# Perceiver layer on one core: attention scores released bank by bank, weighted sums in two parts, a new deal of the key and value steps

## The chip, the cores and the metric

The kernel runs on one core of a Trainium2 chip, as one program. The metric is the device time of one execution in microseconds (us). The engines are named as in the profile: PE is the matrix engine (TensorE; PEld are its weight loads), DVE is VectorE, ACT is ScalarE, POOL is GpSimd, SP is the engine that issues most DMAs.

## What is computed

A layer of three residual parts, of which the change touches the first, cross attention of 64 queries to 1601 context rows in 32 samples, with 16 heads of 16 channels:

```python
q = split_heads(layernorm(x) @ Wq.T + bq)
k = split_heads(ctx @ Wk.T + bk)
v = split_heads(ctx @ Wv.T + bv)
attn = softmax(einsum('bhqd,bhkd->bhqk', q, k) * 4.0)
x = x + merge_heads(einsum('bhqk,bhkd->bhqd', attn, v)) @ Wp.T + bp
```

After it come a cosine circuit with a small feed-forward net and a mixture of seven routed experts and a shared one. They stand in the same program, behind the attention, and the change leaves them alone.

## The kernel before, in words

The attention works in 64 **periods** h, two for each of the 32 samples n = h // 2; a period handles 8 of the 16 heads (m = h % 2). All five engines run their own hand-written list of work for each period, and semaphores tie them together. Each period has four **quads** i = 0 to 3. A quad is what fits into the PSUM tile ps_s at once: four banks j of 128 x 401 scores.

What happens to a quad, engine by engine:

- PE, `scores(h, i)`, L903: 16 small products, which the array runs side by side as 32 x 32 tiles (32 matmul records), fill the four banks. Before the change PE waits until all four banks of the quad before have been read, and signals once.
- DVE, `take_scores`, L648: reads the four banks, scales them into the ring `probs` (5 slots) and leaves each row's extreme in `nmax`.
- After every second quad PE turns these extremes (`turn_max`, L923), DVE reduces them (`reduce_max`, L665), PE spreads the result over the partitions (`spread_max`, L930) and ACT copies it as a bias (`copy_bias`, L468).
- ACT, `exponentials`, L456: four exponentials, one for each bank, with that bias, in place in `probs`.
- DVE, `turn`, L670: one transpose of the quad into `pT`.
- POOL sums the rows (`less_extra`, L325, and `spread_sums`, L337).

When a period's four quads have been turned, PE forms the weighted sums of the values over 13 tiles (`weigh`, L937) and right behind them spreads the sums of the exponentials (L955 to L958, called spread below); DVE then divides (`normalise`, L679). Every fourth period has four normalised halves complete: PE projects them (`project_out`, L960) and DVE adds x and takes row statistics (`residual`, L698).

Meanwhile the keys and values of the next sample are made in 15 **steps** (`step`, L883): 8 K steps of 6 matmuls, 6 V steps of two tiles (12 matmuls) and V12 with one tile. A step fills one of two banks, ACT copies it out (`copy_steps`, L473). `STEP_ORDER` (L33) lists them, `steps_in` (L75) deals them to the four quarters of an even and an odd period. The input of a sample is loaded by SP (`load_ctx`, L239), and split in two parts by POOL (L303, L308). `FIRST_ORDER` and the first 14 steps serve the first sample, before the periods proper.

The order of the work is written out in the `period` functions of each engine: DVE L761, ACT L543, PE L1007, POOL L364, SP L259. On PE, which takes its queue in order, a period before the change reads:

```python
weigh(h - 1)
scores(h + 1, 1); steps[0]          # project_out within, every fourth period
turn_max(2 * h + 2); scores(h + 1, 2); steps[1]
spread_max(2 * h + 2); scores(h + 1, 3); steps[2]
turn_max(2 * h + 3); scores(h + 2, 0); steps[3]
spread_max(2 * h + 3)
```

On DVE a period reads, for i = 0 to 3: take_scores(h + 1, i); residual in i = 1 of every fourth period; turn(h, i); in i = 0 normalise(h - 1); in i = 1 and 3 reduce_max. The turns of i = 2 and 3 also wait for the weighted sums of h - 1, whose slots they use.

Of the kernel before, what the change touches and what calls it, by code (L numbers as in the profile page):

```python
# [16 lines left out]
NC = D // P  # L17
# [15 lines left out]
STEP_ORDER = [K(0, 0), K(0, 1), V(0), K(0, 2), V(2), K(0, 3), V(4), K(1, 0), V(6), K(1, 1), V(8), K(1, 2), V(10), K(1, 3), V(12)]  # L33
# [69 lines left out]
def attention_and_circuit(nc, ctxT, x, wq, bq, wk, bk, wv, bv, wp, rows, ident, marks, x1_scr, x1_mv, x1_by, x1_rs, x1_ex, w1, b1, w2, wr, rb, rows_scr,  # L103
                          wgu, wd, tri, counts):
    with ExitStack() as ctx:
# [132 lines left out]
        def _(sp):  # L238
# [20 lines left out]
            def period(h):  # L259
# [24 lines left out]
            sp.wait_ge(s_filled, HALF * NH)  # L284
# [17 lines left out]
        def _(pool):  # L302
# [13 lines left out]
            def own_queries(n):  # L316

                pool.wait_ge(q_ready_all, NC * (n // 8 + 1))
                if n > 1:

                    pool.wait_ge(s_filled, HALF * 2 * (n - 1))
                for e in range(2):
                    nc.gpsimd.tensor_scalar(q_own[:, n % 2, :, e, :], q_all[:, :, n * SQ:(n + 1) * SQ], mark[:, e:e + 1], None, ALU.mult).then_inc(q_owned, 1)
# [104 lines left out]
            pool.wait_ge(s_filled, HALF * NH)  # L428
# [26 lines left out]
        def _(act):  # L455
            def exponentials(h, i):  # L456
# [5 lines left out]
                for j in range(HALF):  # L462
# [10 lines left out]
            def copy_steps(steps):  # L473

                for n, s in steps:
# [3 lines left out]
                    if kind == "k":  # L479
                        m, q = of  # L480
                        if n > 0:

                            act.wait_ge(s_filled, HALF * (2 * (n - 1) + m + 1))
# [58 lines left out]

            def period(h):  # L543
# [11 lines left out]
                copy_steps(steps[1])  # L555
                if h + 1 < NH:
                    copy_bias(2 * h + 2)
                if h >= 0:
                    exponentials(h, 3)
                for i in ANGLES_IN.get((h, 3), ()):  # L560
                    angles(i)
                copy_steps(steps[2])
                if h + 1 < NH:
                    exponentials(h + 1, 0)
                copy_steps(steps[3])
# [81 lines left out]
        def _(dve):  # L647
            def take_scores(h, i):  # L648
# [3 lines left out]
                dve.wait_ge(s_filled, at + 1)  # L652
# [45 lines left out]
            def residual(t):  # L698
# [5 lines left out]
                nc.vector.tensor_tensor(x_t[:], ps_m[:, D:2 * D], x_t[:], ALU.add).then_inc(x1_ready, 1)  # L704
# [56 lines left out]
            def period(h):  # L761
                for i in range(HALF):
                    if h + 1 < NH:
                        take_scores(h + 1, i)
                    if i == 1 and h % 4 == 0 and h > 0:
# [3 lines left out]
                    if i == 0 and h > 0:  # L769
                        normalise(h - 1)  # L770
                    if i % 2 == 1 and h + 1 < NH:
                        reduce_max(2 * (h + 1) + i // 2)
                    if h == NH - 1:
                        for z in TURNS_IN[i]:
                            if z == 0:
                                dve.wait_ge(s_filled, HALF * NH)
# [99 lines left out]
        def _(pe):  # L876
# [26 lines left out]
            def scores(h, i):  # L903
# [8 lines left out]
                if at > 0:  # L912

                    pe.wait_ge(max_ready, HALF * at)
                else:
                    pe.wait_ge(q_ready_all, NC * NG)
                for g in range(QK):
                    for j in range(HALF):
# [18 lines left out]
            def weigh(h):  # L937

                n, m = h // 2, h % 2
                pe.wait_ge(turned, HALF * (h + 1))  # L940
                pe.wait_ge(kv_copied, STEPS * (n + 1))
                if h > 0:
                    pe.wait_ge(o_normed, h)
                for t in range(KT):
# [9 lines left out]
                mm.then_inc(o_filled, 1)  # L954
# [5 lines left out]
            def project_out(t):  # L960
                pe.wait_ge(o_normed, 4 * t + 4)
                pe.wait_ge(bias_ready, min(8 * t + 10, 2 * NH))
                for e in range(NC):
                    mm = nc.tensor.matmul(ps_m[:, D:2 * D], oT[:, e, :], wp_sb[:, e, :], start=(e == 0), stop=(e == NC - 1))
# [42 lines left out]
            def period(h):  # L1007
                steps = steps_in(h)
                if h > 0:
                    weigh(h - 1)  # L1010
                if h + 1 < NH:
                    scores(h + 1, 1)
                for z in steps[0]:
                    step(*z)
                    if h % 4 == 0 and h > 0 and z == steps[0][0]:
                        project_out(h // 4 - 1)
                if h % 4 == 0 and h > 0 and not steps[0]:
                    project_out(h // 4 - 1)
                if h % 4 == 0 and h > 0:

                    pe.wait_ge(x1_ready, h // 4)
                if h + 1 < NH:
                    turn_max(2 * h + 2)
                    scores(h + 1, 2)
                for z in steps[1]:
                    step(*z)
                if h + 1 < NH:
# [20 lines left out]
            for stage, g in PE_ORDER:  # L1048
                if stage == "weigh":
                    weigh(NH - 1)  # L1050
# [712 lines left out]
```

## Time and profile before

| | us |
|---|---|
| median of 3 runs | 1828.3 (1828.28 to 1830.08) |
| profiled execution, its own time | 1826.5 |
| its span, first to last instruction | 1824.6 |
| attention stage in it | 59 to 1302 |
| mean granted TensorE clock | 0.982 |

Busy over the whole span: PE 1652.9 us (91%), DVE 1566.3 (86%), ACT 1199.9 (66%), POOL 892.4 (49%). In the rows further down a timeline line has the start in us, the duration, engine, line, operation, output<-inputs and the number of instructions merged; a bracket gives the idle time of the engine before it and what ended it. Instructions of one engine overlap, so the distance of two starts, rather than a duration, says what an instruction costs its engine. Names: a_pss holds the scores, a_probs the ring, a_pT the turned quads, a_psm the extremes, a_pso the weighted sums, a_psk and a_psl the two step banks.

### The profile page before, as it was taken

How to read it: one execution, taken by the hardware profiler on the slowest of the kernel's cores; microseconds unless marked ns; L12 is line 12 of the kernel's file. 1: busy time of each engine (PE TensorE's matmuls, PEld its weight loads, DVE VectorE, ACT ScalarE, POOL GpSimd, SP SyncE). 2: the span in 40 equal slices, each digit the busy share in tenths (PEclk: the TensorE clock that was granted, in tenths of full speed). 3: DMA queues.
4: the chain of work that ended last, by engine and by line, in shares of the span. 5: the costliest groups of instructions: out<-in, count | busy, mean ns of one | idle time of the engine just before them, and what ended most of it. 6: DMA issues, size and time to landing. Idle time of an engine off the chain costs nothing. (4 is left out here: it accounts for less than half of the span.)

```text
span 1824.6 us, 59184 instructions
## 1 busy us (share of the span) xinstructions
PE 1652.9 (91%) x24272; PEld 1360.0 (75%) x24272; DVE 1566.3 (86%) x3585; ACT 1199.9 (66%) x3297; POOL 892.4 (49%) x1283
## 2 busy tenths in 40 slices
PE   7999999999999999999999999998499799999998
PEld 4776777767777677677767767766377799999998
DVE  5799999999999999999999999999886766666667
ACT  3676776776776776776776777777565345666652
POOL 5345444445445445444545444443321328888860
PEclk9999999999999999999999999999699899999999
DMA  4111111111111111211111211102012336666633
GB/s 168 40 43 43 64 43 43 61 43 43 64 43 43 61 43 43 64 43 43 62 42 43 64 43 43 53 33 93 6 59 78 136 115 215 211 227 229 214 125 116
DMA packets 43438, 147.86 MB, mean 81 GB/s; under 512 B 5680, under 2 KB 25008, under 8 KB 39712
## 3 DMA queue, kind: packets, MB, share of 16 engines
q1 hardware_dynamic: 38416, 130.71, 21.4%
q0 software_dynamic: 4752, 13.38, 2.4%
q8 instruction: 191, 3.13, 0.7%
q14 instruction: 79, 0.65, 0.1%
HBM read 129.78 MB, written 14.16 MB: 79 GB/s over the span
## 5 line engine op out<-in xcount | busy, mean ns | idle before, releaser
L465 ACT ACTIVATE a_probs<-a_probs,a_bias 128x401 f32<-128x401 f32 x1024 | 632.2, 625 | 0.0
L662 DVE TENSOR_SCALAR_CACHE_REDUCE a_probs<-a_pss 128x401 f32<-128x401 f32 x1024 | 527.8, 572 | 25.5 <-PE a_pss L919 14.9
L677 DVE STREAM_TRANSPOSE a_pT<-a_probs 128x1664 f32<-128x1664 f32 x256 | 487.3, 1904 | 0.0
L333 POOL TENSOR_SCALAR a_ex<-a_probs,a_marks 128x4 f32<-128x4 f32 x256 | 76.4, 299 | 636.7 <-ACT a_probs L465 636.5
L919 PE MATMUL a_pss<-a_keys,a_qown 32*32 32x401 f32 x8192 | 248.0, 509 | 14.2 <-DVE a_probs L662 13.5
L313 POOL TENSOR_TENSOR a_clo<-a_raw,a_chi 128x416 fp32r<-128x416 f32 x240 | 250.2, 1074 | 0.0
L953 PE MATMUL a_pso<-a_pT,a_v 128*32 128x128 f32 x6656 | 199.6, 278 | 10.7 <-DVE a_pT L677 10.7
L465 ACT ACTIVATION_READ_ACCUMULATOR a_probs<-a_probs,a_bias 128x1 f32 x1024 | 197.2, 193 | 0.0
L1592 PE MATMUL e_psg<-e_xh,e_guh 128*128 128x256 f32 x660 | 189.5, 287 | 5.7 <-DVE e_hl L1338 4.2
L953 PEld LDWEIGHTS a_pso<-a_pT,a_v 128*32 128x32 f32 x6656 | 181.7, 112 | 13.0 <-DVE a_pT L677 10.9
L1593 PE MATMUL e_psg<-e_xl,e_guh 128*128 128x256 f32 x660 | 186.6, 283 | 0.0
L1594 PE MATMUL e_psg<-e_xh,e_gul 128*128 128x256 f32 x660 | 186.4, 282 | 0.0
L1528 ACT ACTIVATE e_sg<-e_psg 128x256 f32<-128x256 f32 x180 | 69.1, 384 | 123.8 <-PE e_psg L1594 119.7
L1331 DVE TENSOR_TENSOR e_psg<-e_psg,e_sg 128x256 f32<-128x256 f32 x180 | 77.7, 432 | 80.4 <-ACT e_sg L1528 79.3
L484 ACT ACTIVATE a_keys<-a_psk,a_bk 128x401 f32<-128x401 f32 x131 | 77.4, 591 | 96.9 <-PE a_psk L881 96.9
L484 ACT ACTIVATE a_keys<-a_psl,a_bk 128x401 f32<-128x401 f32 x125 | 73.9, 592 | 95.2 <-PE a_psl L881 95.2
L1592 PEld LDWEIGHTS e_psg<-e_xh,e_guh 128*128 128x128 f32 x660 | 125.6, 190 | 6.4 <-issue 6.4
L1593 PEld LDWEIGHTS e_psg<-e_xl,e_guh 128*128 128x128 f32 x660 | 125.7, 191 | 0.0
L1594 PEld LDWEIGHTS e_psg<-e_xh,e_gul 128*128 128x128 f32 x660 | 125.6, 190 | 0.0
L879 PE MATMUL a_psl<-a_whi,a_chi 128*128 128x256 f32 x428 | 123.6, 289 | 0.0
L880 PE MATMUL a_psl<-a_wlo,a_chi 128*128 128x256 f32 x428 | 120.6, 282 | 0.0
L491 ACT COPY a_v<-a_psl 128x512 f32<-128x512 f32 x99 | 58.0, 586 | 94.9 <-PE a_psl L881 94.9
(246 smaller groups left out, 4299.7 us busy)
## 6 DMA issues: line engine op xcount, KB each, us to landing
a_raw<-in_ctxT SPq DMA_DIRECT2D x60, 832.0 KB, 4.6
f_gur<-in_wgu SPq DMA_DIRECT2D x24, 1408.0 KB, 6.2
f_dr<-in_wd SPq DMA_DIRECT2D x24, 768.0 KB, 4.7
e_big<-ys_scr SPq DMA_DIRECT2D x8, 512.0 KB, 7.7
a_probs<-in_ctxT SPq DMA_DIRECT2D x2, 1664.0 KB, 8.6
a_x<-in_x SPq DMA_DIRECT2D x16, 128.0 KB, 4.5
rows_scr<-f_a SPq DMA_DIRECT2D x8, 256.0 KB, 2.3
rows_scr<-f_a SPq DMA_DIRECT2D x4, 512.0 KB, 3.5
```

Source lines behind the costliest of these rows:

```text
L313: last = nc.gpsimd.tensor_tensor(out=c_lo[:, n % 2, k, cols], in0=src[:, cols], in1=c_hi[:, n % 2, k, cols].bitcast(F32), op=ALU.subtract)
L465: nc.scalar.activation(z, z, ACT.Exp, bias=bias[:, group % 4, at_bias:at_bias + 1], scale=-1.0, accum_out=esum[:, h % 2, j, 2 * e + r:2 * ...
L484: nc.scalar.activation(keys[:, m, q * KG:(q + 1) * KG], step_bank(at)[:, 0:KG], ACT.Identity, bias=bk_sb[:, m:m + 1]).then_inc(kv_copied, 1)
L662: nc.vector.tensor_scalar(probs[:, at % RING, j, 0:KG], ps_s[:, j, 0:KG], -SCALE, None, ALU.mult, ALU.min, accum_out=nmax[:, group % 2, at ...
L677: nc.vector.transpose(pT[:, turned_slot(h, i)].rearrange("p j k -> p (j k)"), probs[:, at % RING].rearrange("p j k -> p (j k)")).then_inc( ...
L879: nc.tensor.matmul(out, a[0], b[0], start=start, stop=False)
L880: nc.tensor.matmul(out, a[0], b[1], start=False, stop=False)
L919: mm = nc.tensor.matmul(ps_s[32 * g:32 * g + 32, j, 0:KG], q_own[32 * j:32 * j + 32, n % 2, m, e, 32 * r:32 * r + 32], keys[32 * j:32 * j ...
L953: mm = nc.tensor.matmul(ps_o[32 * j:32 * j + 32, 0:P], v_of(n)[:, t, 32 * p:32 * p + 32], moving, start=(t == 0), stop=(t == KT - 1))
L1592: nc.tensor.matmul(out, a[0], b[0], start=start, stop=False)
L1593: nc.tensor.matmul(out, a[0], b[1], start=False, stop=False)
L1594: return nc.tensor.matmul(out, a[1], b[0], start=False, stop=stop)
```

## The change

- `scores` goes bank by bank: the order of its loops is swapped, each bank waits only for the reading of the same bank of the quad before, and each bank signals. `s_filled` thus counts four per quad, and all that wait for it count in fours; `take_scores` waits bank by bank.
- `weigh` is split: 8 tiles behind scores 1, 5 tiles and the spread behind scores 2, one quarter later than before for the end.
- `normalise` and `residual` move from quads 0 and 1 to quad 2 on DVE, ahead of the turn; `residual` and `project_out` one period later, and their product to a free half of ps_o.
- `turn_max` moves from ahead of the scores to behind the scores and one step; `spread_max` behind the next scores.
- The steps are dealt 1, 2, 2, 3 and 1, 2, 2, 2 instead of 2, 2, 2, 2 and 2, 2, 2, 1, in a new `STEP_ORDER`.
- ACT does the four exponentials of a quad in two pairs, with a step's copy or the bias copy between them.
- SP stores the residual one period later.

```diff
-STEP_ORDER = [K(0, 0), K(0, 1), V(0), K(0, 2), V(2), K(0, 3), V(4), K(1, 0), V(6), K(1, 1), V(8), K(1, 2), V(10), K(1, 3), V(12)]
+STEP_ORDER = [K(0, 0), K(0, 1), K(0, 2), K(0, 3), V(0), V(2), K(1, 0), V(4), K(1, 1), K(1, 2), K(1, 3), V(6), V(8), V(10), V(12)]
+FIRST_TILES = 8
...
     elif h % 2 == 0:
-        plan = [[(n + 1, 1), (n + 1, 2)], [(n + 1, 3), (n + 1, 4)], [(n + 1, 5), (n + 1, 6)], [(n + 1, 7), (n + 1, 8)]]
+        plan = [[(n + 1, 1)], [(n + 1, 2), (n + 1, 3)], [(n + 1, 4), (n + 1, 5)], [(n + 1, 6), (n + 1, 7), (n + 1, 8)]]
     else:
-        plan = [[(n + 1, 9), (n + 1, 10)], [(n + 1, 11), (n + 1, 12)], [(n + 1, 13), (n + 1, 14)], [(n + 2, 0)]]
+        plan = [[(n + 1, 9)], [(n + 1, 10), (n + 1, 11)], [(n + 1, 12), (n + 1, 13)], [(n + 1, 14), (n + 2, 0)]]
...
-                if h % 4 == 0 and t >= 0:
+                if h % 4 == 1 and t >= 0:
 
                     sp.wait_ge(x1_summed, 2 * t + 2)
                     sp.dma_start(x1_scr[t], x_t[:]).then_inc(x1_free, 16)
...
                 if h >= 0:
-                    exponentials(h, 1)
+                    exponentials(h, 1, FORMER)
                     copy_bias(2 * h + 1)
+                    exponentials(h, 1, LATTER)
                 copy_steps(steps[0])
...
                 if h >= 0:
-                    exponentials(h, 2)
+                    exponentials(h, 2, FORMER)
+                copy_steps(steps[1][:1])
...
+                if h >= 0:
+                    exponentials(h, 2, LATTER)
+                copy_steps(steps[1][1:])
...
-                dve.wait_ge(s_filled, at + 1)
...
+                    dve.wait_ge(s_filled, HALF * at + j + 1)
                     nc.vector.tensor_scalar(probs[:, at % RING, j, 0:KG], ps_s[:, j, 0:KG], -SCALE, None,
...
-                    if i == 1 and h % 4 == 0 and h > 0:
+                    if i == 2 and h > 0:
+                        normalise(h - 1)
+                    if i == 2 and h % 4 == 1 and h > 4:
                         residual(h // 4 - 1)
                     if h >= 0:
                         turn(h, i)
-                    if i == 0 and h > 0:
-                        normalise(h - 1)
...
-                if at > 0:
-
-                    pe.wait_ge(max_ready, HALF * at)
-                else:
+                if at == 0:
                     pe.wait_ge(q_ready_all, NC * NG)
-                for g in range(QK):
-                    for j in range(HALF):
+                for j in range(HALF):
+                    if at > 0:
+
+                        pe.wait_ge(max_ready, HALF * (at - 1) + j + 1)
+                    for g in range(QK):
                         mm = nc.tensor.matmul(ps_s[32 * g:32 * g + 32, j, 0:KG], q_own[32 * j:32 * j + 32, n % 2, m, e, 32 * r:32 * r + 32],
                                               keys[32 * j:32 * j + 32, m, g * KG:(g + 1) * KG], start=True, stop=True)
-                mm.then_inc(s_filled, 1)
+                    mm.then_inc(s_filled, 1)
...
                 steps = steps_in(h)
-                if h > 0:
-                    weigh(h - 1)
+
                 if h + 1 < NH:
                     scores(h + 1, 1)
+                if h >= 0:
+                    spread_max(2 * h + 1)
                 for z in steps[0]:
                     step(*z)
...
+                if h > 0:
+                    weigh(h - 1, range(FIRST_TILES))
+
+                if h + 1 < NH:
+                    scores(h + 1, 2)
+                for z in steps[1][:1]:
+                    step(*z)
                 if h + 1 < NH:
                     turn_max(2 * h + 2)
-                    scores(h + 1, 2)
-                for z in steps[1]:
+                for z in steps[1][1:]:
                     step(*z)
+                if h > 0:
+                    weigh(h - 1, range(FIRST_TILES, KT))
+                    spread(h - 1)
+
                 if h + 1 < NH:
+                    scores(h + 1, 3)
                     spread_max(2 * h + 2)
-                    scores(h + 1, 3)
                 for z in steps[2]:
+                    step(*z)
+
+                if h + 2 < NH:
+                    scores(h + 2, 0)
+                for z in steps[3][:1]:
                     step(*z)
                 if h + 1 < NH:
                     turn_max(2 * h + 3)
-                if h + 2 < NH:
-                    scores(h + 2, 0)
-                for z in steps[3]:
+                for z in steps[3][1:]:
                     step(*z)
-                if h + 1 < NH:
-                    spread_max(2 * h + 3)
```

## Rows read from the trace of the kernel before

**Rows 1.** Busy time by engine in the attention stage; columns as in the first line.
```profile
core 0: us, PE busy (x) PEld busy (x) DVE busy (x) ACT busy (x) POOL busy (x), PEclk, DMA share, GB/s
59.00:1302.00 1243.00, 1127.25 (x20202) 870.05 (x20200) 1166.05 (x2711) 900.35 (x2654) 589.59 (x1016) 0.99 0.16 49
```
**Rows 2.** The same view, four consecutive periods.
```profile
629.47:648.00 18.53, 16.78 (x328) 12.73 (x320) 18.12 (x42) 13.73 (x41) 9.99 (x17) 1.00 0.15 49
648.00:667.96 19.96, 18.80 (x346) 14.90 (x339) 18.13 (x43) 14.44 (x42) 8.82 (x15) 1.00 0.16 51
668.00:686.50 18.50, 16.62 (x328) 12.57 (x313) 18.09 (x43) 13.73 (x41) 9.99 (x17) 1.00 0.16 49
686.50:707.90 21.40, 19.96 (x350) 15.56 (x340) 19.47 (x47) 14.43 (x42) 8.81 (x15) 1.00 0.16 48
```
**Rows 3.** Groups by line, 200 to 1200 us: busy, mean ns | idle before, releasers.
```profile
L687 DVE RECIPROCAL a_sT<-a_pso 128x128 f32<-128x128 f32 x51 | 48.8, 957 | 44.6 <-PE a_pso L953 40.1 <-issue 4.5
```
**Rows 4.** Timeline of DVE, two normalises and part of a period.
```profile
608.08 0.96 DVE L687 RECIPROCAL a_sT<-a_pso 128x128 f32<-128x128 f32 x1 [0.18 <-issue]
...
610.39 0.56 DVE L662 TENSOR_SCALAR_CACHE_REDUCE a_probs<-a_pss 128x401 f32<-128x401 f32 x1
...
629.47 0.96 DVE L687 RECIPROCAL a_sT<-a_pso 128x128 f32<-128x128 f32 x1 [1.60 <-PE a_pso L953]
...
637.81 1.91 DVE L677 STREAM_TRANSPOSE a_pT<-a_probs 128x1664 f32<-128x1664 f32 x1
639.88 0.58 DVE L662 TENSOR_SCALAR_CACHE_REDUCE a_probs<-a_pss 128x401 f32<-128x401 f32 x1 [0.16 <-DVE a_pT L677]
...
641.86 1.91 DVE L677 STREAM_TRANSPOSE a_pT<-a_probs 128x1664 f32<-128x1664 f32 x1
643.69 0.23 DVE L668 TENSOR_REDUCE a_low<-a_psm 8x32 f32<-8x128 f32 x1
```
**Rows 5.** Timeline of PE, the pieces of its queue.
```profile
610.52 1.13 PE L964 MATMUL a_psm<-a_wp,a_oT 128*128 128x256 f32 x4 [0.31 <-DVE a_oT L695]
611.30 0.47 PE L879 MATMUL a_psl<-a_whi,a_chi 128*128 128x256 f32 x1
...
612.81 0.28 PE L881 MATMUL a_psl<-a_whi,a_clo 128*128 128x256 f32 x1
...
625.91 0.24 PE L934 MATMUL a_psm<-a_id,a_low 8*32 8x8 f32 x8
626.08 3.05 PE L953 MATMUL a_pso<-a_pT,a_v 128*32 128x128 f32 x104
628.95 0.40 PE L957 MATMUL a_pso<-a_sin,a_marks 128*32 128x128 f32 x8
629.28 1.10 PE L919 MATMUL a_pss<-a_keys,a_qown 32*32 32x401 f32 x32
...
642.00 0.27 PE L928 MATMUL a_psm<-a_id,a_nmax 128*8 128x128 f32 x1 [1.01 <-DVE a_probs L662]
642.21 0.96 PE L919 MATMUL a_pss<-a_keys,a_qown 32*32 32x401 f32 x32
643.09 0.46 PE L879 MATMUL a_psk<-a_chi,a_whi 128*128 128x416 f32 x1
...
644.44 0.24 PE L934 MATMUL a_psm<-a_id,a_low 8*32 8x8 f32 x8
...
648.71 0.46 PE L879 MATMUL a_psl<-a_chi,a_whi 128*128 128x416 f32 x1
```
**Rows 6.** Timeline of ACT: an exponential, and the copy of a K step.
```profile
613.61 0.63 ACT L465 ACTIVATE a_probs<-a_probs,a_bias 128x401 f32<-128x401 f32 x1
...
650.18 0.60 ACT L484 ACTIVATE a_keys<-a_psl,a_bk 128x401 f32<-128x401 f32 x1 [2.54 <-PE a_psl L881]
```
**Rows 7.** Timeline of POOL: the second part of an input's split.
```profile
629.68 4.17 POOL L313 TENSOR_TENSOR a_clo<-a_raw,a_chi 128x416 fp32r<-128x416 f32 x4
```
**Rows 8.** DMA issues on the page: KB each, us to landing.
```profile
a_raw<-in_ctxT SPq DMA_DIRECT2D x60, 832.0 KB, 4.6
```
**Rows 9.** Timeline of PE's weight loads, those of one quad.
```profile
602.28 0.23 PEld L919 LDWEIGHTS a_pss<-a_keys,a_qown 32*32 32x32 f32 x32
```

More of the change, by code:

```diff
@@ L283, in _ @@
             sp.dma_start(x1[:, NT - 2, :], x1_scr[NT - 2]).then_inc(x1_loaded[group_of[-1]], 16)
-            sp.wait_ge(s_filled, HALF * NH)
+            sp.wait_ge(s_filled, HALF * HALF * NH)
             sp.dma_start(w1_raw, w1).then_inc(loaded, 16)
@@ L319, in own_queries @@
                 if n > 1:
-                    pool.wait_ge(s_filled, HALF * 2 * (n - 1))
+                    pool.wait_ge(s_filled, HALF * HALF * NC * (n - 1))
                 for e in range(2):
@@ L427, in _ @@
             less_extra(NH - 1, 1)
-            pool.wait_ge(s_filled, HALF * NH)
+            pool.wait_ge(s_filled, HALF * HALF * NH)
             pool.wait_ge(o_filled, NC * (B - 1))
@@ L455, in _, with exponentials @@
         def _(act):
-            def exponentials(h, i):
+            def exponentials(h, i, some=range(HALF)):
                 at = HALF * h + i
@@ L461, in exponentials @@
                 act.wait_ge(bias_ready, group + 1)
-                for j in range(HALF):
+                for j in some:
                     z = probs[:, at % RING, j, 0:KG]
@@ L541, in _ @@
             copy_steps([(0, s) for s in range(FIRST_STEPS)])
+            FORMER, LATTER = range(HALF // 2), range(HALF // 2, HALF)
             def period(h):
@@ L558, in period @@
                 if h >= 0:
-                    exponentials(h, 3)
+                    exponentials(h, 3, FORMER)
+                copy_steps(steps[2][:1])
+                if h >= 0:
+                    exponentials(h, 3, LATTER)
                 for i in ANGLES_IN.get((h, 3), ()):
                     angles(i)
-                copy_steps(steps[2])
+                copy_steps(steps[2][1:])
                 if h + 1 < NH:
-                    exponentials(h + 1, 0)
-                copy_steps(steps[3])
+                    exponentials(h + 1, 0, FORMER)
+                copy_steps(steps[3][:1])
+                if h + 1 < NH:
+                    exponentials(h + 1, 0, LATTER)
+                copy_steps(steps[3][1:])
             for h in range(-1, NH):
@@ L775, in period @@
                             if z == 0:
-                                dve.wait_ge(s_filled, HALF * NH)
+                                dve.wait_ge(s_filled, HALF * HALF * NH)
                             round_turns(z)
@@ L935, in spread_max, with weigh @@
                 mm.then_inc(max_spread, 1)
-            def weigh(h):
+            def weigh(h, some):
                 n, m = h // 2, h % 2
-                pe.wait_ge(turned, HALF * (h + 1))
-                pe.wait_ge(kv_copied, STEPS * (n + 1))
-                if h > 0:
-                    pe.wait_ge(o_normed, h)
-                for t in range(KT):
+                if some.start == 0:
+                    pe.wait_ge(turned, HALF * (h + 1))
+                    pe.wait_ge(kv_copied, STEPS * (n + 1))
+                    if h > 0:
+                        pe.wait_ge(o_normed, h)
+                    if h % 4 == 1 and h > 4:
+                        pe.wait_ge(x1_ready, (h - 1) // 4)
+                for t in some:
                     for j in range(HALF):
@@ L953, in weigh, with spread @@
                         mm = nc.tensor.matmul(ps_o[32 * j:32 * j + 32, 0:P], v_of(n)[:, t, 32 * p:32 * p + 32], moving, start=(t == 0), stop=(t == KT - 1))
-                mm.then_inc(o_filled, 1)
+                if some.stop == KT:
+                    mm.then_inc(o_filled, 1)
+            def spread(h):
                 pe.wait_ge(sums_spread, h + 1)
@@ L961, in project_out @@
                 pe.wait_ge(o_normed, 4 * t + 4)
-                pe.wait_ge(bias_ready, min(8 * t + 10, 2 * NH))
                 for e in range(NC):
-                    mm = nc.tensor.matmul(ps_m[:, D:2 * D], oT[:, e, :], wp_sb[:, e, :], start=(e == 0), stop=(e == NC - 1))
+                    mm = nc.tensor.matmul(ps_o[:, D:2 * D], oT[:, e, :], wp_sb[:, e, :], start=(e == 0), stop=(e == NC - 1))
                 mm.then_inc(y_filled, 1)
@@ L1049, in _ @@
                 if stage == "weigh":
-                    weigh(NH - 1)
+                    weigh(NH - 1, range(KT))
+                    spread(NH - 1)
                     pe.wait_ge(loaded, 16 * 7)
```

16 lines of the change are left out of this document (6 added, 10 removed).

## The prediction

> **What bounds the kernel now.** I read the busy time of the long middle stretch first. It is the attention stage, 59 to 1302 us: VectorE (DVE) is busy for 1166 of its 1243 us, TensorE (PE) for 1127, ScalarE for 900 [rows 1]. Two engines lie within a few per cent of the bound, so neither can lose time without the other noticing. Next I cut four periods out of the middle, from one normalise to the next: 18.53, 19.96, 18.50 and 21.40 us, 78.39 together, with the granted clock at 1.00, 2.4 GHz [rows 2]. This pattern repeats to the end of the stage. Then I asked the groups where DVE's idle time lies: nearly all in front of the reciprocal that opens normalise, 44.6 us in 1000 [rows 3]. The timeline shows how: it waits 1.60 us in one period and 0.18 in the next, in turn [rows 4].
>
> **The DVE's own work.** From the timeline [rows 4], with t = 0 where the last bank of a quad of scores has been read and the turn starts: turn to reduce 1.83 (641.86 to 643.69), reduce 0.23, reading four banks 1.98 to 1.99 (639.88 to 641.86), turn directly to a reading 2.06 to 2.07 (637.81 to 639.88), normalise 2.31 (608.08 to 610.39). The new order in a period is read, turn, read, turn, reduce, read, normalise, turn, read, turn, reduce: 1.99 + 2.06 + 1.99 + 1.83 + 0.23 + 1.99 + 2.31 + 2.06 + 1.99 + 1.83 + 0.23 = 18.51 without waiting. Residual adds 21.40 - 19.96 = 1.44 to every fourth period [rows 2]. So moving normalise and residual removes no work: all that can change is what DVE waits for.
>
> **PE's pieces**, start to start [rows 5]. A quad of scores takes 0.88 (642.21 to 643.09); a K step before work of another tile shape 1.35 (643.09 to 644.44); a V step after other work 1.51 to its twelfth matmul (611.30 to 612.81) and, an estimate from K's last matmuls, 0.12 more to the next step or 0.19 to 0.2 to another shape, so 1.63 or 1.70. V12 has six of the twelve: about 1.00. Turn_max 0.21 (642.00 to 642.21), spread_max 0.17 to 0.19, the weighted sums 2.87 for 13 tiles (626.08 to 628.95), so 1.77 for eight and 1.10 for five, spread 0.33, project_out 0.78. Hand-overs: PE starts 0.14 after DVE's last read (641.86 [rows 4], 642.00); DVE starts normalise 0.52 after spread's start (628.95, 629.47), and reduce 0.39 after turn_max's (its 0.27 and the same 0.12).
>
> **Does this bookkeeping hold?** Tried on the kernel before: t = 0, turn_max 0.14, scores 0.35, one K step 1.23, spread_max 2.58, weigh 2.76, spread 5.63, normalise could start at 6.15; DVE reaches it at 1.83 + 0.23 + 1.99 + 1.91 = 5.96. Wait 0.19, seen 0.18. With K and V in that quarter everything is 1.5 later and the wait is 1.6, seen 1.60 [rows 4]. It gives both periods to a few hundredths.
>
> **The change, walked through.** Decisive is PE's new queue between the scores that wait for quad 3 and the spread that normalise needs. PE runs in order. *Odd period* (t = 0 as above): scores' last bank starts at 0.14; the next step 0.81 later (an estimate: a quad's 0.88 to 0.90 less the hundredths that issuing three banks takes), K10 at 0.95; turn_max 2.30; V4 2.50; K11 4.13; scores of quad 1 at 5.38, spread_max 6.28, K12 6.47; eight tiles of weigh 7.82; scores of quad 2 at 9.69; K13 10.59; turn_max 11.94; V6 12.14; five tiles 13.84; spread 14.94. DVE: reduce is due at 1.83 but can start at 2.69, a wait of 0.86 that before was none, since turn_max then stood ahead of the scores. Read, turn, read, turn: due at the second reduce at 10.79, turn_max gives 12.33, wait 1.54. Then reading ends at 14.55, spread gives 15.46, wait 0.91. Sum 3.31, period 18.51 + 3.31 = 21.82. *Even period*: last bank 0.14, V12 0.95, turn_max 1.95 (reduce waits 0.51), K00 2.15; PE is ready for quad 1 at 3.50 but its last bank is read only at 4.56; so K01 at 5.70, weigh 7.05, quad 2 at 8.92, K02 9.82, turn_max 11.17 (reduce waits 1.12), K03 11.37, five tiles 12.72, spread 13.82 (normalise waits 0.56). Sum 2.19, period 20.70. Where project_out stands ahead of weigh, 0.85 with its change of shape comes onto this path; residual adds its 1.44, so that period is 24.11. Four periods: 21.82 + 20.70 + 24.11 + 20.70 = 87.33, against 78.39: 8.94 more.
>
> After normalise comes the other side of the bad deal: DVE needs 2.31 + 2.06 + 1.99 before quad 3 is read, while PE has one quad, spread_max and two steps, about 4.2, and then idles; nothing of the weighted sums can be pulled into that hole.
>
> **Edits with no price.** *Bank-wise signals*: the last bank is filled as late as before (0.14 behind its read). Three more waits per quad on either engine: between 0 and about 0.08 each (a reading's accumulator pass exposed); taken as 0, since a turn, which waits too, follows a read at the banks' own pace (0.50). If the upper end held on the path, +30 us; if spread_max ran wholly under the scores, 0.19 a period less, -12. *Exponentials in twos*: the same instructions of 0.63 [rows 6]; a K copy can start 1.47 after its step (648.71 [rows 5] to 650.18). The tightest turn is quad 1's in the odd period: its last exponentials, now behind the bias copy, end near 8.6, its reading at 8.96. Cover 0.4; without it, the 1.54 wait behind would absorb more. Quad 3's is covered by about 2. *K00 of the next sample*: its split input comes from POOL's 4.17 us after quad 1's exponentials [rows 7], some 10 us earlier. *SyncE*: the store of a residual now stands behind one more input load and in front of the next; that next load goes out about 6 us later than its buffer allows, near 21 of 24, and with 4.6 to land [rows 8] it is there 2 us before POOL asks. Covered; otherwise POOL alone would slip.
>
> **Weighing a rule.** The new order of a bank sends four matmuls in a row to the same 32 rows of the array. Before, the fifth load already goes to rows in use: all 32 loads are over within 0.23 us while the matmuls run on to 0.96 [rows 5, 9], so loads do run under matmuls of their own rows. I take 0.88 for a quad. The Trainium skill, "TensorE: Matmul & The Clock Gate", section "Part 3: Packing small matmuls", says that a weight load overlaps matmuls in flight only when they use another row group. By it every bank would be serial; the trace disagrees.
>
> **The sum.** Full periods are h = 1 to 61: 61/4 x 8.94 = 136 us. The first two periods lack the sums, the last two the steps (there turn_max directly follows the scores and nothing waits longer): +-4. The stages after 1302 don't change. The profiled execution took 1826.5 (span 1824.6): 1962.5; the median of the runs is 1.8 above it: 1964.
>
> **Rivals.** (1) *Faster*: DVE never waits, because bank-wise starts put PE ahead. Place: spread must start before 12.15 - 0.52 = 11.63 after t = 0 (DVE's own work to the normalise). PE has 14.8 of work ahead of it, so it would need some 3.2 us of it to run beneath other work, as if steps didn't wait for scores to drain. Then four periods take 4 x 18.51 + 1.44 = 75.5, -2.9: -44 us, 1784. Against: the step starts 0.88 behind the scores. 4%. (2) *No change*: bank by bank is idle, and later sums and later normalise cancel: 1828. Against: 12.5 to 14.8 us of PE work must fit into 11.5. 3%. (3) *Milder*: steps run shorter or spread_max and the split sums hide, a third to two thirds of the loss: 1870 to 1915. The bookkeeping above speaks against it. 7%. (4) *Packing breaks*: four matmuls of about 0.5 one behind another in each bank, banks side by side: +1.2 a quad, five a period, +290: 2250 at least, more if banks are serial too. Against: [rows 9]. 2%. It is what that rule of the Trainium skill would do. (5) *Worse waiting*: each bank's wait costs on both engines, or the granted clock, 1.00 (2.4 GHz) in all four periods [rows 2], falls to its lower level with PE's longer idling: above 2005. 5%. The forecast has the remaining 79%.
>
> **Numbers.** 1964. Range 1905 to 2005: from the walk's bounds (about 1930 to 2000) out to the upper part of the milder case. What a measurement here can tell from no change is about 0.2%, 4 us. Slower 93%, the same 3%, faster 4%.
>
> **What the profile after should show.** Periods of about 20.7 and 21.8 in turn, 24.1 every fourth; the attention stage near 1379 us; DVE's share of it down from 94 to about 85%. In front of reduce, where before shows no wait [rows 4], some 125 to 140 us over the run, ended by turn_max; in front of the reciprocal still about 45, now in every period. Quads as dense as before. PE idle in front of the scores of quad 0. Wrong would be: reduce not waiting, normalise waiting less than 0.3 on average, or a quad longer than 1 us without a wait.

## The result, and the profile after

The changed kernel takes 1905.3 us (median of 4 runs, 1902.8 to 1907.0) against 1828.3 before: a ratio of 1.042, 95% interval 1.040 to 1.044. Slower by 77 us, as forecast in sign, where 136 were forecast. The profiled execution shown here took 1902.76 us, with a span of 1900.9.

The windows, first the attention stage, then four periods from normalise to normalise (they answer to [rows 1, 2]):

```profile
core 0: us, PE busy (x) PEld busy (x) DVE busy (x) ACT busy (x) POOL busy (x), PEclk, DMA share, GB/s
61.57:1376.95 1315.38, 1252.92 (x20190) 922.04 (x20166) 1140.09 (x2710) 894.76 (x2646) 590.95 (x1015) 0.97 0.14 47
...
777.36:797.80 20.44, 20.00 (x346) 15.27 (x338) 17.66 (x42) 14.31 (x42) 9.42 (x17) 1.00 0.15 51
797.80:817.10 19.30, 18.86 (x328) 13.11 (x321) 17.67 (x42) 13.73 (x41) 9.47 (x17) 1.00 0.14 48
817.10:838.42 21.32, 20.88 (x350) 16.04 (x342) 17.67 (x43) 14.31 (x42) 9.42 (x17) 1.00 0.08 34
838.42:859.19 20.77, 18.87 (x328) 13.11 (x320) 19.03 (x47) 13.73 (x41) 9.46 (x17) 1.00 0.20 61
```

The stage went from 1243 to 1315 us and carries 72 of the 76 us between the two spans. Four periods at full clock take 81.83 instead of 78.39 [rows 2], 3.44 more; over 61 periods that is 61/4 x 3.44 = 52 us. The clock of the whole stage fell from 0.99 to 0.97, while these four periods show 1.00: the other 20 us of the stage go with stretches at a lower clock, which the first experiment tests. Look also at DVE: 17.66 us of work in a period where before had 18.1, although the change was to take no work from it.

The waits of DVE over the whole span (total, times, longest):

```profile
DVE a_low L684 <- PE a_psm L944: 130.2, 126, 8.2
...
DVE a_sT L703 <- PE a_pso L973: 34.3, 60, 0.7
```

The new wait is where it was forecast: reduce (a_low) waits for turn_max in every period, 130.2 us in all (forecast 125 to 140). That the sum falls into the forecast is luck, as the account below shows. The reciprocal (a_sT) waits in all periods instead of every second one.

Now one odd period on PE, the one that has project_out. The quad of scores that begins at 821.56 runs with DVE's reads, bank by bank; the last read that it waits for ends at 822.82, where the DVE lines below begin. That is t = 0 of the prediction's walk.

```profile
821.56 2.27 PE L935 MATMUL a_pss<-a_keys,a_qown 32*32 32x401 f32 x32 [0.44 <-DVE a_probs L678]
823.76 0.46 PE L895 MATMUL a_psl<-a_chi,a_whi 128*128 128x416 f32 x1
...
825.02 0.27 PE L944 MATMUL a_psm<-a_id,a_nmax 128*8 128x128 f32 x1
825.04 0.36 PE L895 MATMUL a_psk<-a_whi,a_chi 128*128 128x256 f32 x1
...
826.55 0.36 PE L895 MATMUL a_psl<-a_chi,a_whi 128*128 128x416 f32 x1
...
827.81 0.96 PE L935 MATMUL a_pss<-a_keys,a_qown 32*32 32x401 f32 x32
828.50 0.45 PE L950 MATMUL a_psm<-a_id,a_low 8*32 8x8 f32 x8
828.88 0.46 PE L895 MATMUL a_psk<-a_chi,a_whi 128*128 128x416 f32 x1
...
830.14 1.03 PE L987 MATMUL a_pso<-a_wp,a_oT 128*128 128x256 f32 x4
831.09 1.95 PE L973 MATMUL a_pso<-a_pT,a_v 128*32 128x128 f32 x64
832.98 0.97 PE L935 MATMUL a_pss<-a_keys,a_qown 32*32 32x401 f32 x32
833.88 0.46 PE L895 MATMUL a_psl<-a_chi,a_whi 128*128 128x416 f32 x1
...
835.15 0.27 PE L944 MATMUL a_psm<-a_id,a_nmax 128*8 128x128 f32 x1
835.17 0.36 PE L895 MATMUL a_psk<-a_whi,a_chi 128*128 128x256 f32 x1
...
836.78 1.30 PE L973 MATMUL a_pso<-a_pT,a_v 128*32 128x128 f32 x40
837.89 0.40 PE L981 MATMUL a_pso<-a_sin,a_marks 128*32 128x128 f32 x8
```

And what DVE does in it (turn, the two reduces, normalise, residual's first add):

```profile
822.82 1.91 DVE L693 STREAM_TRANSPOSE a_pT<-a_probs 128x1664 f32<-128x1664 f32 x1
...
825.33 0.28 DVE L684 TENSOR_REDUCE a_low<-a_psm 8x32 f32<-8x128 f32 x1 [0.60 <-PE a_psm L944]
...
835.46 0.28 DVE L684 TENSOR_REDUCE a_low<-a_psm 8x32 f32<-8x128 f32 x1 [2.04 <-PE a_psm L944]
...
838.42 0.96 DVE L703 RECIPROCAL a_sT<-a_pso 128x128 f32<-128x128 f32 x1 [0.71 <-PE a_pso L973]
839.41 0.48 DVE L707 SCALAR_TENSOR_TENSOR a_op<-a_pso,a_marks,a_sT 128x64 f32<-128x64 f32 x2
839.92 0.29 DVE L711 SCALAR_TENSOR_TENSOR a_oT<-a_op,a_bv 128x64 f32<-128x64 f32 x1
840.13 0.42 DVE L717 TENSOR_TENSOR a_x<-a_x,a_bp 128x256 f32<-128x256 f32 x1
```

Three things are to be seen. Normalise waits for the spread at 837.89, which stands behind PE's whole queue, in the order that was walked. The step of V behind turn_max starts 0.02 after it (825.02, 825.04; 835.15, 835.17), where the walk had 0.20, and then takes 1.61 up to the weighted sums (835.17 to 836.78), where the walk had 1.70. And normalise takes 840.13 - 838.42 = 1.71, where the walk had 2.31. The whole difference there is its last instruction, shown by the groups from 200 to 1200 us (busy, mean ns | idle before it):

```profile
L711 DVE SCALAR_TENSOR_TENSOR a_oT<-a_op,a_bv 128x64 f32<-128x64 f32 x48 | 13.8, 287 | 1.7
```

The same group of the kernel before:

```profile
L695 DVE SCALAR_TENSOR_TENSOR a_oT<-a_op,a_bv 128x64 f32<-128x64 f32 x51 | 45.5, 892 | 1.8
```

892 ns before, 287 after, for the same instruction. The timeline of before shows what ran beside it: POOL's split of an input, four instructions of 1.04.

```profile
608.29 4.16 POOL L313 TENSOR_TENSOR a_clo<-a_raw,a_chi 128x416 fp32r<-128x416 f32 x4
...
609.58 0.89 DVE L695 SCALAR_TENSOR_TENSOR a_oT<-a_op,a_bv 128x64 f32<-128x64 f32 x1
```

POOL's second instruction ends near 608.29 + 2.08 = 610.37, and the DVE instruction, begun about a quarter of the way into it, ends at 609.58 + 0.89 = 610.47, some 0.1 behind it. By the single records it is 0.08 to 0.09 in each of the 52 periods from 200 to 1250 us that have such a split. The two instructions ahead of it, which read one operand from PSUM, keep their 0.48. In the changed kernel normalise comes two quads later, when POOL is through with the split: no period there has the two side by side.

The lower clock is the other finding. The windows around one hole of PE:

```profile
1007.60:1009.50 1.90, 0.03 (x1) 0.00 (x0) 1.79 (x4) 1.90 (x6) 1.19 (x3) 1.00 0.79 216
1009.50:1011.30 1.80, 1.76 (x30) 0.64 (x32) 1.80 (x7) 0.26 (x2) 0.36 (x1) 1.00 0.80 318
1011.30:1014.70 3.40, 3.40 (x20) 2.53 (x11) 2.13 (x5) 0.94 (x3) 0.00 (x0) 0.51 0.00 0
1014.70:1025.50 10.80, 10.80 (x223) 7.60 (x238) 9.50 (x27) 7.92 (x25) 7.30 (x12) 1.00 0.11 23
```

PE stands idle for 1.90 us ahead of the scores of quad 0, while DVE does normalise, residual, a turn and reads; it works again from 1009.5, and from 1011.3 to 1014.7 the granted clock is 0.51, the 1.2 GHz level. Such a hole comes in every fourth period. Leaving out the last 35 us of the stage, where the steps have run out and both kernels fall to the lower level, the trace holds 18 stretches at that level, 68.3 us together (called low stretches below); the trace of before holds none. Not every hole is followed by one: behind 11 of the 14 holes a low stretch begins 0.8 to 3.0 us after work has resumed, behind three there is none, and seven low stretches lie further from any hole.

### The profile page after: what moved, and what is told of

It reads as the page before. It is cut to its first block and busy times, and to the rows that moved or that the text cites. A ratio compares the mean times of both kernels' runs of the same rounds, so it can differ in the third digit from the quotient of the medians.

```text
span 1900.9 us, 59183 instructions
## 1 busy us (share of the span) xinstructions
PE 1785.4 (94%) x24272; PEld 1417.8 (75%) x24272; DVE 1541.1 (81%) x3585; ACT 1197.6 (63%) x3297; POOL 893.6 (47%) x1283
## 5 line engine op out<-in xcount | busy, mean ns | idle before, releaser
L935 PE MATMUL a_pss<-a_keys,a_qown 32*32 32x401 f32 x8192 | 366.2, 514 | 52.1 <-DVE a_probs L678 51.4
L935 PEld LDWEIGHTS a_pss<-a_keys,a_qown 32*32 32x32 f32 x8192 | 98.1, 103 | 189.6 <-DVE a_probs L678 108.7
L973 PE MATMUL a_pso<-a_pT,a_v 128*32 128x128 f32 x6656 | 212.9, 279 | 7.3 <-DVE a_pT L693 7.3
L684 DVE TENSOR_REDUCE a_low<-a_psm 8x32 f32<-8x128 f32 x128 | 35.6, 278 | 130.3 <-PE a_psm L944 130.2
L895 PE MATMUL a_psl<-a_whi,a_chi 128*128 128x256 f32 x412 | 128.3, 311 | 0.0
L895 PE MATMUL a_psk<-a_whi,a_chi 128*128 128x256 f32 x420 | 127.4, 303 | 0.0
```

What stands on the lines that cost most here:

```text
L895: nc.tensor.matmul(out, a[0], b[0], start=start, stop=False)
L973: mm = nc.tensor.matmul(ps_o[32 * j:32 * j + 32, 0:P], v_of(n)[:, t, 32 * p:32 * p + 32], moving, start=(t == 0), stop=(t == KT - 1))
```

## The experiments

Theory: the 77 us are 52 at full clock, from PE's queue in front of the waits of reduce and normalise (already less what the change gains unasked where normalise leaves POOL's split), plus some 20 of the lower clock that goes with the holes. Rivals: bank by bank costs the time itself; the pairs of exponentials do; the lower clock changes nothing that counts. Periods named below run from the turn of one quad 3 to that of the next (t = 0 of the walk); they are odd, even, odd with residual, the medians at full clock. The changed kernel has 20.45, 19.30, 22.78.

**Fill the hole.** In the periods with residual, four products into an unused part of ps_m ahead of the scores of quad 0:

```diff
+                if h % 4 == 1 and h > 4:
+                    pe.wait_ge(bias_ready, 2 * h + 3)
+                    for _ in range(4):
+                        nc.tensor.matmul(ps_m[:, D:2 * D], a_id_sb[:], wp_sb[:, 0, :], start=True, stop=True)
                 if h + 2 < NH:
                     scores(h + 2, 0)
```

> The changed kernel with four extra matmul calls on PE (their product is used by nobody) in the 1.9 us hole ahead of quad 0's scores, in the periods with a residual. Theory (the stretches at 1.2 GHz that the changed kernel shows follow these holes and cost some 20 us): about 10 or fewer such stretches remain instead of 21, and 1880 to 1895. Rival (they lie off the path or have another cause): 1905, or a few us more where the filler delays the scores.

1885.6 us, ratio 1.031 (1.029 to 1.032): 19.7 us faster than the change, with more work. The periods at full clock stay at 20.45, 19.30 and 22.78; of the 18 low stretches 4 are left, 13.7 us, and no hole of 0.9 us or more. The clock from 330 to 1330 us, first of this kernel and then of the changed one:

```profile
330.00:1330.00 1000.00, 981.50 (x15826) 719.70 (x15825) 877.47 (x2096) 682.35 (x2022) 455.04 (x779) 1.00 0.15 47
```

```profile
330.00:1330.00 1000.00, 960.96 (x15358) 710.62 (x15357) 862.05 (x2060) 671.89 (x1986) 450.22 (x768) 0.97 0.14 47
```

So filling the holes takes away 54.6 us at the lower level and 19.7 us of time, with the periods at full clock unchanged: the holes bring most of the low stretches about, those further off included, and a microsecond at the lower level costs about 0.36 us here. The 57 us that are left are the 52 at full clock and what the four remaining stretches cost. What brings those four about is not shown.

**Deal two steps behind the spread.** K03 and V6 go from ahead of the last five tiles to the quarter behind them; everything else stays:

```diff
-        plan = [[(n + 1, 1)], [(n + 1, 2), (n + 1, 3)], [(n + 1, 4), (n + 1, 5)], [(n + 1, 6), (n + 1, 7), (n + 1, 8)]]
+        plan = [[(n + 1, 1)], [(n + 1, 2)], [(n + 1, 3), (n + 1, 4), (n + 1, 5)], [(n + 1, 6), (n + 1, 7), (n + 1, 8)]]
-        plan = [[(n + 1, 9)], [(n + 1, 10), (n + 1, 11)], [(n + 1, 12), (n + 1, 13)], [(n + 1, 14), (n + 2, 0)]]
+        plan = [[(n + 1, 9)], [(n + 1, 10)], [(n + 1, 11), (n + 1, 12), (n + 1, 13)], [(n + 1, 14), (n + 2, 0)]]
```

> The changed kernel with one step of each period (K03, V6) dealt behind spread instead of ahead of it. Main theory: odd periods 20.45 to about 19.7, even ones 19.30 to about 18.85, PE's idle time ahead of quad 0's scores shrinks; about -37 us, and up to 20 more if fewer stretches run at the lower clock: 1850 to 1870. Rival (late turn_max): its wait stays, so within 10 us of 1905. Rival (bank-wise signals cost): 1905.

1845.9 us, ratio 1.009 (1.008 to 1.011), 4 us below what was expected: the largest part of the loss is gone with one step a period, the same work in another place. Periods 19.65, 18.77, 21.98; four of them 79.17, 2.66 less, which is 40 us over the stage; and the hole is filled too, with 4 low stretches left, the other 20. The reciprocal's wait is gone from the list; reduce still waits:

```profile
DVE a_low L684 <- PE a_psm L944: 110.7, 126, 6.8
```

PE's queue in front of the spread is the cause of what normalise waited.

**Turn_max ahead of the scores**, as in the kernel before, with the rest of the change kept:

```diff
                 if h + 1 < NH:
+                    turn_max(2 * h + 2)
                     scores(h + 1, 2)
-                for z in steps[1][:1]:
-                    step(*z)
-                if h + 1 < NH:
-                    turn_max(2 * h + 2)
-                for z in steps[1][1:]:
+                for z in steps[1]:
                     step(*z)
...
```

> The changed kernel with turn_max put back ahead of the scores in quads 2 and 0, all else as changed. Main theory (the path from the reading of quad 3 over PE's queue to spread, then normalise, turn and reading on DVE sets each period): the wait in front of reduce, 130 us, vanishes, but spread comes no earlier (0.4 later in odd periods, 0.05 earlier in even ones), so the time moves to the reciprocal: +5 to +20 us against the changed kernel's 1905. Rival (the late turn_max itself is what costs): 1775 to 1845.

1933.0 us, ratio 1.057 (1.055 to 1.058), 28 us slower than the change, where 5 to 20 were expected. Its waits of DVE:

```profile
DVE a_sT L703 <- PE a_pso L973: 108.4, 60, 2.2
...
DVE a_pT L693 <- ACT a_probs L466: 54.1, 49, 2.0
...
DVE a_low L684 <- PE a_psm L944: 11.2, 17, 4.6
```

The wait of reduce goes, 130.2 to 11.2, as the walk says; but it comes back in front of normalise (34.3 to 108.4) and of turns that wait for exponentials (54.1), since PE, which now waits for the reads of the quad before it turns, gets to the spread hardly sooner: 14.47 after t = 0 in odd periods (14.21 in the change), 12.91 in even ones (13.07). Periods are 20.71, 19.14 and 23.03, four of them 82.02, 0.19 more, which is 3 us; and low stretches double to 34, 133 us. So turn_max's place alone is not the loss, and what DVE waits at is only the last visible end of PE's queue. By the price of the first experiment (19.7 us for 54.6) the added 65 us at the lower level would cost some 23 us, an estimate; with the 3 that leaves about 2 of the 28.

**One wait for each quad** on PE and DVE, with the change's order of banks:

```diff
+                dve.wait_ge(s_filled, HALF * (at + 1))
-                    dve.wait_ge(s_filled, HALF * at + j + 1)
...
+                if at > 0:
+                    pe.wait_ge(max_ready, HALF * at)
-                    if at > 0:
-                        pe.wait_ge(max_ready, HALF * (at - 1) + j + 1)
```

> The changed kernel with one wait per quad instead of one per bank, on PE and on DVE (the order of the matmuls and the number of signals stay as changed). Main theory: the last bank is what the path waits for, so bank by bank is worth 0.1 in the step behind quad 0 and, in even periods, the 0.2 of spread_max that now hides in the wait: +5 to +20 us on 1905, more if PE's idle time grows and the clock falls oftener. Rival (the four waits per quad cost): 10 to 40 us faster.

1937.1 us, ratio 1.059 (1.057 to 1.061), 32 us slower than the change and more than expected. Periods 20.68, 19.80 and 23.00, four of them 83.28, 1.45 more: 22 us; the low stretches rise to 25, 95.6 us, which by the same price would make the other 10. The waits by bank are worth about 0.36 a period here and cost nothing that shows: the rival that they are the loss falls.

**Exponentials in fours**, ACT's order as before the change:

```diff
-                    exponentials(h, 1, FORMER)
+                    exponentials(h, 1)
                     copy_bias(2 * h + 1)
-                    exponentials(h, 1, LATTER)
...
```

> The changed kernel with all four exponentials of a quad in a row, as before, and the copies of the steps behind them. Main theory: ScalarE is covered by 0.4 us at the tightest turn, so the pairs are worth nothing: 1905 +-5. Rival (a step's copy that comes 1.2 us later holds PE's next step but one, or a turn): +10 to +60 us.

1908.2 us, ratio 1.041 (1.038 to 1.045), against 1.042: no effect that can be measured (the two kernels' runs overlap), and the same three periods. In the change the pairs are idle.

**POOL's split.** In both kernels the second half of the split goes behind the sums of quad 2. That takes it away from normalise in the kernel before, and puts it beside normalise in the changed one:

```diff
                 less_extra(h, 1)
+                less_extra(h, 2)
                 if n + 2 < B:
                     ctx_low(n + 2, k, raw[:])
-                less_extra(h, 2)
```

In the kernel before:

> The kernel before, with POOL's 4.2 us split of an input put behind quad 2's sums instead of quad 1's, so that it no longer runs beside normalise. Theory (normalise took 2.31 us before and takes 1.71 in the changed kernel because its last instruction, 0.89, ran beside that split): that instruction falls to 0.28 and, DVE being the bound there, the time by 0.6 a period: 1785 to 1795. Rival (its length has to do with what follows it on DVE): no change, 1828. Rival (PE bounds anyway): the instruction shrinks, the wait at the reciprocal grows, 1828.

1795.8 us, ratio 0.982 (0.980 to 0.984): 1 us above what was expected and 33 us faster than before by one call moved past another on an engine that is busy half the time. Normalise's last instruction takes 285 ns at the median, the periods are 17.93, 19.35, 17.93 and 20.8, which is 2.38 less for four, 0.60 each.

In the changed kernel:

> The changed kernel with the edit that took the split away from normalise in the kernel before: here it puts the split beside normalise (quad 2's sums end near 13 of a period, normalise runs from about 13.6 or 14.8). Theory: normalise's last instruction rises from 0.28 to 0.89, and as normalise lies on the path here, each period by 0.6: +30 to +40 us, 1935 to 1950. Rival (the gain of that edit in the kernel before had another cause): 1905.

1960.1 us, ratio 1.071 (1.069 to 1.073): 55 us slower than the change, above what was expected. The odd period pays 0.80, the one with residual 1.71, the even one 0.03 only (21.25, 24.49, 19.33; the one with residual always ends at the lower level, but takes 24.49 to 24.50 however late that begins). The timeline has the reason, an even and an odd normalise with the split beside each:

```profile
588.99 3.15 POOL L314 TENSOR_TENSOR a_clo<-a_raw,a_chi 128x416 fp32r<-128x416 f32 x3
590.87 0.31 DVE L711 SCALAR_TENSOR_TENSOR a_oT<-a_op,a_bv 128x64 f32<-128x64 f32 x1
...
610.08 4.18 POOL L314 TENSOR_TENSOR a_clo<-a_raw,a_chi 128x416 fp32r<-128x416 f32 x4
612.21 1.10 DVE L711 SCALAR_TENSOR_TENSOR a_oT<-a_op,a_bv 128x64 f32<-128x64 f32 x1
613.24 1.31 DVE L717 TENSOR_TENSOR a_x<-a_x,a_bp 128x256 f32<-128x256 f32 x1
```

The POOL instructions end 1.05 apart: at 591.09 in the even period, and DVE's ends at 591.18; at 613.22 in the odd one, and DVE's ends at 613.31. The one came late in a POOL instruction and hardly waited, the other came at its beginning and waited through it. Residual's first add, also of two operands in SBUF, then waits through the fourth: 1.31 instead of 0.42, which makes the 1.71 of that period (0.80 + 0.90). Four periods make 2.57 more, 39 us. The remaining 16 go with the low stretches, 30 of them now, 157 us; that these cost the 16 is argued, and by the price of the first experiment they would have cost twice that.

The Trainium skill, "SBUF — State Buffer", section "Who interferes with whom", says that a VectorE instruction with two SBUF inputs contends with a GpSimd instruction that reads SBUF, over a pair of ports that is an exclusive lock. The trace agrees: the DVE instruction is not slowed by a share, but ends 0.08 to 0.09 behind POOL's instruction, whether it began 0.08, 0.26 or 0.85 into it.

**A version that takes the sums early**: all 13 tiles and the spread right behind scores 1, normalise and residual at quad 1, the deal of before, POOL's split behind quad 2's sums; the banks and the pairs of the change stay:

```diff
                 if h + 1 < NH:
                     scores(h + 1, 1)
                 if h >= 0:
                     spread_max(2 * h + 1)
-                for z in steps[0]:
-                    step(*z)
...
                 if h > 0:
-                    weigh(h - 1, range(FIRST_TILES))
+                    weigh(h - 1, range(KT))
+                    spread(h - 1)
+                for z in steps[0]:
+                    step(*z)
+                if h + 1 < NH:
+                    turn_max(2 * h + 2)
...
```

> A version made of what the runs showed: the changed kernel with the whole weighted sums and spread right behind the scores of quad 1, normalise and residual in quad 1 on DVE, turn_max ahead of the scores again, the steps dealt as in the kernel before, and POOL's split behind quad 2's sums. Theory: spread starts 5.6 or 8.0 after the last read of quad 3 instead of 13.1 or 14.2, normalise is due at 8.1, and DVE waits 0.45 at most: periods of 17.9 to 18.4 and 1.5 more with a residual, 1750 to 1775 us. Rival (PE's own work of about 17.8 a period sets the time once DVE doesn't wait): 1780 to 1800, with the waits at the readings of quads 2 and 3.

1858.7 us, ratio 1.017 (1.015 to 1.018): a miss by 84 us. The low clock is nearly gone (0.99 from 330 to 1280 us), but a new wait is there:

```profile
DVE a_pT L693 <- ACT a_probs L466: 67.0, 107, 1.5
```

The turns wait for the exponentials: with the pairs, the second pair of a quad stands in ACT's queue behind the copy of a step, and in this order the step is late. What was idle in the change costs here. So the same kernel with the four exponentials in one go:

> The version n1_sums_early, in which turns waited 67 us for exponentials that stood behind a step's copy, with the exponentials in fours ahead of the copies, as in the kernel before. If that order was what failed in it, the waits of the turns vanish and the periods come to 17.9 to 18.6: 1755 to 1800. If instead PE's work bounds it, the waits move to the readings of the scores and the time stays above 1830.

1804.4 us, ratio 0.987 (0.986 to 0.989), just above what was expected. The turns' waits have left the list. The longest of the attention stage that remains is

```profile
DVE a_sT L690 <- PE a_pso L960: 42.6, 60, 1.9
```

It is 101 us below the change with the banks and their waits kept: the loss goes with the order and the deal of PE's work and with normalise's place behind it. It beats both kernels, but not the kernel before with POOL's split moved alone (1795.8): with the sums early, the change's other parts bring nothing more.

**The kernel before, split moved and one step dealt earlier.** There normalise still waits in every second period because K and V steps stand ahead of weigh; in even periods one goes forward:

```diff
-        plan = [[(n + 1, 1), (n + 1, 2)], [(n + 1, 3), (n + 1, 4)], [(n + 1, 5), (n + 1, 6)], [(n + 1, 7), (n + 1, 8)]]
+        plan = [[(n + 1, 1), (n + 1, 2), (n + 1, 3)], [(n + 1, 4), (n + 1, 5)], [(n + 1, 6), (n + 1, 7)], [(n + 1, 8)]]
```

> The version b2_pool_later (1796 us), with the steps of the even periods dealt 3, 2, 2, 1 instead of 2, 2, 2, 2, so that one K step and not a K and a V step stands between the reading of quad 3 and the weighted sums. Theory (the path from quad 3's reading to spread decides): the wait of 1.60 at the reciprocal in every second period falls to 0.2 to 0.7, while quads 2 and 3 may come 0.3 late: -20 to -40 us, 1755 to 1776. Rival (PE has no slack in the quarter that takes the third step): its lateness passes on and the time stays within 5 us of 1796.

1766.9 us (1764.7 to 1768.2), ratio 0.966 (0.964 to 0.968): 61 us faster than before, 138 faster than the change. Four periods, the first with residual:

```profile
729.04:748.68 19.64, 19.50 (x350) 15.21 (x343) 18.87 (x47) 14.30 (x42) 7.77 (x16) 1.00 0.15 53
748.68:766.61 17.93, 16.66 (x328) 12.62 (x320) 17.52 (x43) 13.62 (x41) 11.45 (x19) 1.00 0.15 51
766.61:785.08 18.47, 18.47 (x346) 14.51 (x337) 17.52 (x42) 14.30 (x42) 8.16 (x15) 1.00 0.17 56
785.08:803.01 17.93, 16.66 (x328) 12.62 (x321) 17.52 (x42) 13.62 (x41) 10.84 (x19) 1.00 0.17 50
```

Two periods stand at 17.93, close to 18.51 - 0.60: DVE's own work in the prediction's sum, less what the split had cost. Reciprocal's wait over the span, 52.0 before and 57.1 with the split moved alone, falls to

```profile
DVE a_sT L687 <- PE a_pso L953: 23.2, 36, 4.3
```

## Why the prediction was right in sign and too high in size

- **The mechanism held.** "Decisive is PE's new queue between the scores that wait for quad 3 and the spread that normalise needs": the trace runs in that order, reduce and normalise wait where it said, DVE's share of the stage is 1140/1315 = 87% (85 forecast), and PE's holes in front of quad 0 came, though of some length only in the periods with residual (1.90; 0.44 ahead of the quad at 821.56). Dealing one step behind the spread took back 59 of 77 us.
- **Luck: reduce's 130.2 us in the 125 to 140 forecast.** At full clock reduce waits 0.60 and 1.18 in odd periods (2.04 with project_out) and 0.16 and 0.74 in even ones. Four periods make 6.22, which is 95 us over the 61 periods, where the walk had 0.86, 1.54, 0.51 and 1.12 and 0.85 more with project_out, 136 us. The sum was filled up by longer waits at the lower clock and by two waits ahead of the first period, 8.2 and 5.3.
- **Every period was walked 1.33 to 1.40 too long**: 21.82, 20.70, 24.11 against 20.45, 19.30, 22.78; four of them 87.33 against 81.83. That is 5.50 x 61/4 = 84 us too much. Two terms of the sum carry it.
- **The first failed term: "moving normalise and residual removes no work", with normalise at 2.31.** It measured 1.71. The 2.31 was read correctly from [rows 4], but 0.61 of it was a block by POOL's instruction, which the move leaves behind. The two POOL runs show it in either direction. That is 0.6 x 61 = 37 of the 84 us.
- **The second: turn_max as a change of tile shape on both sides** (K before it 1.35, turn_max 0.20, V behind it 1.63 to 1.70). In the period shown K before it takes 1.26 (823.76 to 825.02), turn_max 0.02, V 1.51 between steps and 1.61 ahead of the tiles. A V step straight behind a K step takes 1.51 up to another shape in the kernel before, lines that the walk had not used:

```profile
615.65 0.28 PE L879 MATMUL a_psl<-a_whi,a_chi 128*128 128x256 f32 x1
...
617.16 0.24 PE L934 MATMUL a_psm<-a_id,a_low 8*32 8x8 f32 x8
```

So the 128 x 8 tile costs the run of 128 x 128 products about 0.1 in all, not a change of shape twice. The spread starts 15.07 after t = 0 in the period shown, where the walk with its 0.85 for project_out had 15.79; without project_out it is 14.21 at the median, where the walk had 14.94; so normalise starts 0.7 earlier. The 0.20 had been read where turn_max is followed by scores of 32 x 32 tiles [rows 5], and it does cost that there. In even periods the spread starts at 13.07 instead of 13.82: there V12 takes 0.82 where the walk had 1.00, and spread_max runs under the wait for a bank's read, an upper end that the prediction had named and not taken. These are most of the other 47 of the 84 us.
- **The third error went the other way and hid part of the first two**: the granted clock was priced only as a rival of 5%, together with the bank waits, and as a way to be above 2005; in the sum it stood at nothing. It falls behind most of the holes of every fourth period and costs some 20 us. Without it the forecast would have been off by 77 - 20 = 57 against 136.
- **Right at no price**: the waits by bank (without them it is 22 us more at full clock, so they gained a little), the pairs of exponentials (no difference), and the density of quads: 0.90 from one to the next step (832.98 to 833.88), with four matmuls in a row on the same rows. The rival of broken packing, 1.2 more a quad, did not come.
- **The range.** 1905 was its low end, and the median lies on it. The milder rival, "steps run shorter or spread_max and the split sums hide", was nearer the truth than its 7%: its first half, shorter steps, is the second term here.

Left open: what brings about the low stretches that lie far from any hole, why those of the run with POOL's split beside normalise cost less, and whether the full clock could be kept without added products in this order. No run kept all of the change with both turn_max and the steps put back; the nearest is the version with the sums early and the exponentials in fours. That the 2.31 hides a block was argued from the ends of instructions and shown by moving the split; no run took POOL's operands out of SBUF.

## What to carry to other kernels

In an in-order queue, walk the work that stands between the last read that releases it and the result that the critical engine waits for; one step a period moved across that line was worth 40 us here at full clock. Before pricing an instruction at what it takes now, look for the same instruction's shortest duration in the trace, and at what ran beside the long ones: the place of one call on an engine off the path was worth 33 us with one sign in one kernel and 55 with the other in the next. Where a change makes holes on PE, read the granted clock behind them as a term of its own.

## What was not expected of the hardware

A VectorE instruction of 128 x 64 with both operands in SBUF went from 0.28 to 0.89 and to 1.10 us beside POOL's tensor_tensor, always ending 0.08 to 0.09 behind the POOL instruction under way; its neighbours with an operand in PSUM kept 0.48 for two. A product with a 128 x 8 tile between 128 x 128 products delayed the next one by 0.02, and the step behind it by 0.1 in all. And PE's granted clock went to 0.51 for 3.4 us or 6.8, 0.8 to 3.0 us after work had resumed, behind 11 of 14 holes of 1.9 us or a little more.
